# A two-layer graph kernel: the second layer loads stored lane one-hots, GpSimd casts them, six bins of seven are added as pairs

## The reference

```python
# layer 0: 6250 nodes x 128 channels, 200000 edges, sorted by dst
e   = leaky_relu(concat(x[src], x[dst]) @ w, 0.2) @ a
att = exp(e) / segment_sum(exp(e), src)[src]
x   = layernorm(x + segment_sum(x[src] * att, dst))
# layer 1: 4 heads of 32 channels
H   = x @ W                                   # per head
s   = leaky_relu(H_s[src] + H_t[dst], 0.2)    # H_s, H_t: H against A_left, A_right
s   = exp(s - max(s));  alpha = s / (segment_sum(s, src)[src] + 1e-8)
agg = segment_sum(alpha * H[dst], src) + x @ residual_projection
x   = layernorm(x + elu(agg))
```

## Time and profile before

| | |
|---|---|
| three runs | 3257.14, 3259.38, 3259.60 us; median 3259.38 |
| the profiled execution | span 3274.5 us; nothing around it is recorded apart |
| PE / DVE / ACT / POOL busy in that span | 3060.7 / 3045.9 / 2750.1 / 155.0 us |
| score stage | to 1317 us |
| layer 1 | 2227 to 3221 us, a block of 7 steps in 20.11 us |

### The profile page before, as it was taken

The page is one execution under the profiler, slowest core; times in us unless marked ns, Lnnn a source line. Parts: engine busy times, 40 slices in busy tenths (PEclk is TensorE's granted clock), DMA queues, the critical chain, the costliest instruction groups (busy, mean ns, idle before and its releaser), DMA issues. The chain is left out here.

```text
span 3274.5 us, 101508 instructions
## 1 busy us (share of the span) xinstructions
PE 3060.7 (93%) x40072; PEld 2792.8 (85%) x40072; DVE 3045.9 (93%) x4921; ACT 2750.1 (84%) x6946; POOL 155.0 (5%) x249
## 2 busy tenths in 40 slices
PE   5777699999999999699999999989999999999996
PEld 4666677778777877699999999988999999999994
DVE  8999889999999997799999999989999999999997
ACT  6988888888888885799999999987888888888887
POOL 0000000000000000000000000000111111111110
PEclk9989899999999997799999999999999999999998
DMA  3000022222222222234333333334455545554541
GB/s 66 13 14 11 23 98 93 87 93 94 93 87 93 94 86 48 65 96 97 97 97 96 97 96 97 97 93 137 161 163 160 164 161 163 161 163 161 162 151 41
DMA packets 173823, 333.06 MB, mean 102 GB/s; under 512 B 54876, under 2 KB 109616, under 8 KB 173264
## 3 DMA queue, kind: packets, MB, share of 16 engines
q1 hardware_dynamic: 170996, 323.30, 32.5%
q10 hardware_dynamic: 2348, 3.20, 0.4%
HBM read 320.77 MB, written 5.66 MB: 100 GB/s over the span
## 5 line engine op out<-in xcount | busy, mean ns | idle before, releaser
L1009 PE MATMUL l_gathered<-xp,l_src_onehot 128*128 128x128 bf16 x7203 | 467.0, 221 | 11.2 <-DVE l_src_onehot L922 11.2
L1436 PE MATMUL l_gathered<-hp,l_onehot 128*128 128x128 bf16 x7203 | 458.5, 219 | 0.0
L704 PE MATMUL sc_z<-sc_onehot,pq 128*128 128x256 f32 (+1 forms) x2450 | 429.4, 298 | 23.3 <-DVE sc_leaky L617 18.3
L1009 PEld LDWEIGHTS l_gathered<-xp,l_src_onehot 128*128 128x128 bf16 x7203 | 407.9, 99 | 26.3 <-DVE l_src_onehot L922 11.7
L788 ACT ACTIVATE sc_leaky<-sc_z 128x1024 f32<-128x1024 f32 (+3 forms) x325 | 309.8, 953 | 143.3 <-PE sc_z L708 140.5
L617 DVE SCALAR_TENSOR_TENSOR sc_leaky<-sc_z,sc_leaky 128x1024 f32<-128x1024 f32 (+3 forms) x325 | 370.1, 1139 | 60.0 <-ACT sc_leaky L788 52.5
L847 DVE TENSOR_TENSOR l_lane<-iota_b,l_lane_pairs 128x896 bf16<-128x896 bf16 x686 | 421.0, 614 | 0.0
L1436 PEld LDWEIGHTS l_gathered<-hp,l_onehot 128*128 128x128 bf16 x7203 | 406.1, 98 | 0.4
L708 PE MATMUL sc_z<-sc_onehot,pq 128*128 128x256 f32 (+1 forms) x2450 | 400.9, 286 | 0.0
L1450 PE MATMUL l_acc<-e,l_lane_wide 128*128 128x132 f32 x2744 | 385.5, 283 | 0.3 <-ACT e L1514 0.3
L704 PEld LDWEIGHTS sc_z<-sc_onehot,pq 128*128 128x128 f32 x2450 | 344.6, 196 | 35.9 <-issue 34.5
(11 more groups left out here) (246 smaller groups left out, 6107.4 us busy)
## 6 DMA issues: line engine op xcount, KB each, us to landing
rows_got<-edge_rows_wide SPq DMA_DIRECT2D x338, 448.0 KB, 3.7
l_got<-edge_rows_src SPq DMA_DIRECT2D x343, 224.0 KB, 3.2
placed<-edge_rows SPq DMA_DIRECT2D x144, 512.0 KB, 3.7
out_dram<-X SPq DMA_DIRECT2D x12, 256.0 KB
S<-edge_rows_wide SPq DMA_DIRECT2D x5, 448.0 KB, 8.4
edge_rows<-e SPq DMA_DIRECT2D x98, 6.1 KB
edge_rows_wide<-e SPq DMA_DIRECT2D x98, 12.2 KB
sc_last_rows<-edge_rows SPq DMA_DIRECT2D x24, 64.0 KB, 3.5
```

What stands on the lines that cost most here:

```text
L704: nc.tensor.matmul(z[:, b, 0:nw, :], PQ[:, b0 + b, q, 0:C], hot[:, r % HOTS, b, 0, 0:nw, :], start=(b == u and q == 0), stop=False)
L1009: ins = nc.tensor.matmul(gps[:, t % 2, i * P:(i + 1) * P], hot[:, t % RING, i, :], parts[:, g * GX + i, q, :], start=(q == 0), stop=(q == 2))
L1436: ins = nc.tensor.matmul(gps[:, t % 2, i * P:(i + 1) * P], dst_hot[:, t % RING, i, :], hp[:, g * GX + i, q, 0:C], start=(q == 0), stop=(q ...
```

## The change

Three things are changed together. The score stage stores its lane one-hots: its comparisons are regrouped (both blocks of a pair for the same 7 bins stand together in one of two buffers, `LANES = 2`), and ACT issues a DMA of each group to `lane_rows` in DRAM, 448 KB for a pair. A buffer is compared into again when its store has landed. To make room, small tiles of that stage move into other tensors. Layer 1 loads these rows (224 KB a step, four buffers, from SP's queue) in place of `find_lanes` on DVE, and POOL casts them in place of ACT. `SPLIT` is 6: one bin is added in float32, six as pairs, so `take_high` and `take_low` cover 792 elements where they covered 396. DVE does `take_low` a step later, and PE gathers two steps ahead where it gathered one.

```diff
--- score_edges
-    HOTS, EARLY, RING, LANES = 3, 3, 4, 3
+    HOTS, EARLY, RING = 3, 3, 4                     # LANES = 2
...
                 def lane_hot(pair, i):
-                    if c >= LANES:
-                        dve.wait_ge(s["added"], c - LANES + 1)
+                    if o == 0 and group >= LANES:
+                        dve.wait_ge(s["added"], items_through(group - LANES))
+                        dve.wait_ge(k.lanes_stored[group % LANES], 16 * (group // LANES))
...
+                def store_lanes(pair, g):
+                    group, nw = pair * 7 + g, (2 if pair < PAIRS - 1 else 1)
+                    act.wait_ge(s["lane_hot"], items_through(group))
+                    act.dma_start(lane_rows[GX * g:GX * g + GX, :, 2 * pair:2 * pair + nw, :].rearrange("b p n l -> p b n l"),
+                                  ohs[:, group % LANES, :, 0:nw, :]).then_inc(k.lanes_stored[group % LANES], 16)
...
                     if 1 <= r <= R:
                         positive(r - 1)
+                    for pair, g in groups_due(r - 1):
+                        store_lanes(pair, g)
--- layer1, SP
+                def load_lanes(t):
+                    b, g = divmod(t, PER)
+                    if t >= LOADS:
+                        sp.wait_ge(s["lane_wide"], t - LOADS + 1)
+                    sp.dma_start(lane[:, t % LOADS], lane_rows[b, :, GX * g:GX * g + GX, :]).then_inc(arrived[t % LOADS], 16)
--- layer1, DVE
-                for t in range(-AHEAD - 1, R):
+                for t in range(-AHEAD, R + 1):
...
-                    if 0 <= t + 1 < R:
-                        find_lanes(t + 1)
+                    if t >= 1:
+                        take_low(t - 1)
...
-                    if t >= 0:
-                        take_low(t)
--- layer1, POOL
-                for b in range(NB):
-                    (all-reduce of b, add_low(b - 1), lowering of X[b])
+                def widen(t):
+                    pool.wait_ge(arrived[t % LOADS], 16 * (t // LOADS + 1))
+                    if t >= 2:
+                        pool.wait_ge(s["added"], t - 1)
+                    pool.wait_ge(s["hot"], min(t + AHEAD, R - 1) + 1)
+                    nc.gpsimd.tensor_copy(lane_wide[:, t % 2], lane[:, t % LOADS]).then_inc(s["lane_wide"], 1)
+
+                for t in range(R):
+                    b, g = divmod(t, PER)
+                    if g == PER - 2 and b + 1 < NB:
+                        find_all(b + 1)
+                    widen(t)
+                    if g == 4 and b >= 1:
+                        add_low(b - 1)
+                    if g == 1:
+                        lower(b)
--- layer1, PE
-                    if 0 <= t + 1 < R:
-                        gather(t + 1)
+                    if 0 <= t + 2 < R:
+                        gather(t + 2)
```

More of the change, by code:

```diff
@@ L533, in score_edges, with rest_of @@
         cps = nps[:, 511:512]
+        def rest_of(pair):
+            first, nw = min(2 * pair + 2, NB), (2 if pair < PAIRS - 1 else 1)
+            return e0[:, first:first + nw, 0:NB]
         def bytes_of(r):
@@ L537, in bytes_of @@
             at = step % 2 * 4 * R_BYTES
-            chunk = got[:, step // 2 % 2, at:at + w * R_BYTES] if step < PER - 1 else last_got[:]
+            chunk = got[:, step // 2 % 2, at:at + w * R_BYTES] if step < PER - 1 else last_got
             return chunk.rearrange("p (b a n l) -> p b a n l", a=2, n=2, l=P)
@@ L556, in den_items, with lane_group, items_through, groups_due @@
         def den_items(pair):
-            return [(o, 7 * g) for o in range(2 if pair < PAIRS - 1 else 1) for g in range(7)]
+            return [(o, 7 * g) for g in range(7) for o in range(2 if pair < PAIRS - 1 else 1)]
+        def lane_group(pair, i):
+            return pair * 7 + (i // 2 if pair < PAIRS - 1 else i)
+        def items_through(group):
+            pair, g = divmod(group, 7)
+            return pair * DEN + (2 * g + 2 if pair < PAIRS - 1 else g + 1)
+        def groups_due(r):
+            return [(pair, g) for pair in range(PAIRS) for g in range(7)
+                    if slots(pair)[1][2 * g + 1 if pair < PAIRS - 1 else g] == r]
         DEN = 14
@@ L596, in _ @@
                         sp.wait_ge(s["hot"], last_group_step(pair - 1, 6) + 1)
-                    load_score_rows(sp, k, rows, pair, 6, 1, last_got[:], last_loaded)
+                    load_score_rows(sp, k, rows, pair, 6, 1, last_got, last_loaded)
             @block.vector
@@ L1266, in layer1 @@
         src_hot, dst_hot = hot[:, 0:2], hot[:, 2:]
-        win = sb("lane_pairs", [P, 2, NB, 2], BF16)
+        arrived = [ctx.semaphore(f"l1_lanes_arrived{h}") for h in range(LOADS)]
         absent, never, exp_ready = sb("absent", [P, 2, NB], BF16), sb("never", [P, P], BF16), sb("exp_ready", [P, 1])
@@ L1284, in _ @@
                     load_rows(sp, k, got, S, wide_rows, u)
+                    if u == LOADS_1 + AHEAD_1:
+                        for h in range(len(k.lanes_stored)):
+                            sp.wait_ge(k.lanes_stored[h], 16 * k.lane_stores[h])
+                        for t in range(LOADS - 1):
+                            load_lanes(t)
+                    if u >= AHEAD + 2:
+                        load_lanes(u - AHEAD - 2 + LOADS - 1)
+                for t in range(R - AHEAD - 2 + LOADS - 1, R):
+                    load_lanes(t)
             @block.vector
@@ L2445, in gnn_program @@
         k.score_rows = [ctx.semaphore(f"score_rows{h}") for h in range(2)]
+        k.lanes_stored = [ctx.semaphore(f"lanes_stored{h}") for h in range(LANES)]
+        k.lane_stores = [len(range(h, 7 * PAIRS, LANES)) for h in range(LANES)]
         k.rows_ahead = [ctx.semaphore(f"rows_ahead{h}") for h in range(AHEAD_1)]
```

112 lines of the change are left out of this document (53 added, 59 removed).

## The result

The changed kernel takes 3736.66 us (median of four, 3728.5 to 3745.9) against 3259.4 before: ratio 1.147, interval 1.145 to 1.148. It is slower, as forecast, but 477 us slower where 126 were forecast, outside the range.

The account below looks back on a forecast made before the run. PE was taken to bound layer 1, busy all 20.11 us of a block. The forecast was 3259.4 + 115 (PE waiting behind POOL's switches, less its saving) + 14 (score stage), about 3385 us, range 3200 to 3530.

Parts of the forecast that it names:

- The deciding step: Layer 1, POOL: two library switches a block delay queued casts, PE waits 1.4 and 2.3 us; +115 us over 49 blocks.
- The size of the switch: POOL in layer 1: one library switch, called X, taken as 5.7 us; its case covered 5 to 7.4.
- Case (d): Layer 1, POOL: a longer switch of 7.4 us, waits 3.1 and 4.0, block 25.9, 3555 us; upper end of the 0.47 case.
- PE's sum: Layer 1, PE: with SPLIT = 6 a step of scores, gather and sums takes 2.67 us, a block 18.76.
- The cast: Layer 1, POOL: a cast takes 0.95 us, between bounds of 0.90 and 3.2.
- rival (c): Layer 1, POOL: a slow cast of 2.0 us makes POOL's queue 27.5 a block, +362, 3635 us; chance 0.07.
- Rival (b): Layer 1: port contention of POOL's cast with DVE's subtraction, steps 2.95 to 3.0, block 21.2, 3345 us; chance 0.14.
- The score stage: Score stage: DVE's waits for store landings cost 7 us within pairs and about 7 at the end, together +14.
- by a steady share: Whole kernel: the profiled execution, 3274.5 us, is 15.1 over the median by a steady share, so differences add to the median.
- X: Layer 1, POOL: length of one library switch; at X = 4.4 gain and loss cancel, the no-change case, chance 0.08.

Follow-up runs that it names:

- Run 1: The changed kernel with add_low moved to DVE and the lowering of X to ACT, so POOL has only all-reduces and casts: 3356.65 us, ratio 1.030 to before.
- run 2: The changed kernel with the casts back on ACT; POOL keeps its three small jobs and both switches a block: 3461.12 us, ratio 1.062 to before.
- run 12: The changed kernel without switches, with three l_lane_wide buffers, a wider score-stage end, POOL casting five bins of seven and ACT two: 3212.05 us, ratio 0.986 to before.
- run 5: The changed kernel with casts on ACT, POOL's jobs in the old order and ACT's take two steps earlier: 3263.87 us, ratio 1.0014 to before.
- Run 8: The kernel before with SPLIT = 6 alone (no stored rows, comparison on DVE, casts on ACT): 3477.07 us, ratio 1.069 to before.
- run 3: The changed kernel, switches kept, with three buffers of l_lane_wide instead of two: 3653.81 us, ratio 1.122 to before.
- run 4: The changed score stage with its stores, and layer 1 as in the kernel before: 3279.99 us, ratio 1.006 to before.

## Why the prediction was right and wrong

- **The deciding step was right in kind**: two switches a block, with casts queued behind them, stop PE, where two buffers leave it 4.8 us. Run 1, which takes away the switches and leaves the casts, gives back 380 of 477 us.
- **The size of the switch was the step that failed first.** I took 5.7, close under the shortest late gap of 5.99, against two direct rows of 7.40 and 8.64. Measured: 7.9 and 7.5. The 5.99 bounded that one gap and not the mean: in run 2 single gaps ahead of the all-reduce go from 5.8 to 8.1. Case (d), with 7.4, had the waits of PE at 7.1 a block; they are 7.3. It forecast a block of 25.9 and 3555 us. By the 5.95 of the Trainium skill (GPSIMD Engine Reference, section 2.1, Instruction dispatch) the forecast would have been an estimated 3410; that section speaks of a first call, while here the gap comes back twice in every block, and no run here shows so short a mean gap (6.8 in run 2, its shortest).
- **A term was missing: the clock.** The prediction priced each wait by its own length, but 32 of 34 waits brought matmuls at half the granted clock (0.50, gather 2.40 for 1.33); over layer 1 it was 0.83. PE's work of 17.9 us took 22.0, which is 4.1 a block or 201 us. The block is 17.9 of work, 7.4 idle and 4.1 by the clock, together 29.4, where case (d) had 18.8 and 7.1. The term is read from the trace; no run changes the clock alone.
- **PE's sum was too high.** It had 2.67 a step; without a wait and at full clock it is 2.56 in the changed kernel and 2.57 in run 12. Six pairs take 0.82 where six times 0.153 were taken. That is 0.9 a block or some 44 us, which hid part of the clock's cost. That a step of run 12 takes 2.67 is chance: DVE sets it.
- **A second wait was missed**: the all-reduce, late by its switch, holds up the weights. In the changed kernel it overlaps the waits for casts (DVE waited 46.7 us of 500 for l_weight); runs 2 and 5 price it without casts on POOL, at 197 us.
- **The cast** was taken at 0.95: 1.01, and 0.93 undisturbed. The one-input price of 0.57 for 128 elements was start and not rate, as argued; rival (c) is out.
- **Rival (b), port contention**, was right as a second layer under the switches: its steps of 2.95 to 3.0 are 500 / 162 = 3.09 in run 1. That its total of 3345 lies so near the 3357 is partly luck, since seven such steps are 20.7 to 21.0 and not 21.2. That the subtraction suffers beside a cast and the weighing, which reads PSUM, does not, held in all runs. The subtraction alone is 0.97 (0.96 forecast).
- **The score stage** was forecast at +14 and is +21: 11.7 at the end instead of 7, 3.7 in the pairs from 500 to 1300 us; the stores landed in 3.4 us (median). The rest is the clock at its end. The prediction took the profile of before to lie 15 us over the median "by a steady share"; it lies there in this one place (last section).
- Two slips of the sum changed nothing: 3259.4 + 115 + 14 is 3388 and not 3385, and at X = 4.4 a block is 19.9 and not 20.1.
- The chances: slower had 0.68. Range and point failed because the price of the longer gaps, 7.4, was called the upper end of a case instead of its middle, and because no case let the clock fall.

## What to carry to other kernels

A gap called "issue" ahead of an instruction on POOL is a price; when work that others wait for is put into the same queue, take the gaps that show the price openly, not the ones that only bound it. To an engine at its limit add what a wait sets off: TensorE came back at half clock here, so waits of 7.4 us a block cost 11.5. And where two engines disturb each other, place the work: the same cast cost 0 to 0.6 us a step by what it lay beside, and a wait that placed it was worth 71 us.

## What was unexpected of the hardware

- The gap of a switch was not constant: 6.8 to 7.3 on the mean with nothing behind it (run 2), 7.5 to 7.9 in the changed kernel, 8.65 to 9.0 with three buffers. What lengthens it stays open, and so does what fills it: the trace has no instruction there, and the page of the changed kernel counts 316 and 161 packets on the two instruction queues, that of run 1, without switches, 316 and 159. "Library switch" is the prediction's name for it.
- TensorE's clock fell to half near the end of the score stage in every execution profiled, but from moments between 1260 and 1298 us. In the profile of before it fell at 1263:

```profile
1250.00:1260.00 10.00, 10.00 (x103) 7.97 (x102) 9.54 (x16) 7.39 (x12) 0.00 (x0) 1.00 0.34 54
1260.00:1270.00 10.00, 9.33 (x82) 6.35 (x81) 6.43 (x12) 4.62 (x10) 0.00 (x0) 0.63 0.17 26
1270.00:1280.00 10.00, 10.00 (x84) 8.78 (x84) 6.34 (x12) 3.66 (x8) 0.00 (x0) 0.50 0.26 42
```

  Run 8 has the same score stage as before. Its clock fell at 1293, and the stage took 893 us for 912:

```profile
1270.00:1280.00 10.00, 10.00 (x127) 8.35 (x125) 8.93 (x18) 8.25 (x25) 0.00 (x0) 1.00 0.50 79
```

  So the profile of before lay 15 us over its median by the clock, which blurs what the stores cost. With a late fall in both, run 3 (1298 us, 910 for the stage, stores and all) is 16.5 over run 8; with an early one in both, run 4 is 10.2 over before. What decides the moment is not shown: PE's last wait ahead of the fall in the profile of before, of 0.67, stands at the same place in run 8, where the clock stayed up.
